# Merge, router norm and gate of a graph-attention router moved into the dense experts' program

## What is computed

```python
h = (x_flat @ W_gat).reshape(M, HEADS, NUM_EXPERTS)
a_src = (h * att_src).sum(-1)
a_dst = (h * att_dst).sum(-1)
e = jax.nn.leaky_relu(a_src[src] + a_dst[dst], negative_slope=0.2)
e_max = jax.ops.segment_max(e, dst, num_segments=M)
ee = jnp.exp(e - e_max[dst])
denom = jax.ops.segment_sum(ee, dst, num_segments=M)
alpha = ee / (denom[dst] + 1e-16)
msg = h[src] * alpha[:, :, None]
agg = jax.ops.segment_sum(msg, dst, num_segments=M).reshape(M, HEADS * NUM_EXPERTS) + b_gat
scores = _layernorm(agg, ln_gamma, ln_beta).reshape(M, HEADS, NUM_EXPERTS).mean(1)
topk_s, topk_i = jax.lax.top_k(scores, TOP_K)
w = jax.nn.softmax(topk_s, axis=-1)
for ei in range(NUM_EXPERTS):
    g = jnp.where(topk_i == ei, w, 0.0).sum(-1)
    hh = jax.nn.gelu(x @ W1[ei] + b1[ei], approximate=False)
    out = out + g[..., None] * (hh @ W2[ei] + b2[ei])
```

## Time and profile before

| what | us |
|---|---|
| median of 3 runs | 3600.15 (3591.07 to 3607.87) |
| span of the profiled execution, first to last instruction | 3135.8 |
| last copy of a dense output starts | 1534.97 |
| first VectorE instruction of the merge that needs own | 1582.93 |
| merge's last multiplies start | 1595.23 |
| router norm starts | 1602.31 |
| gate starts | 1610.19 |
| gate's last instruction starts | 1615.35 |

### The profile page before, as it was taken

One profiled execution on the slowest core, in us unless ns is written; L12 is line 12 of the kernel. 1 busy time (PEld: TensorE's weight loads), 2 busy tenths in 40 slices (PEclk: granted clock), 3 DMA queues, 4 the chain that ended last, 5 costly groups with the idle time before them and its releaser, 6 DMA issues. The chain is left out here.

```text
span 3135.8 us, 49560 instructions
## 1 busy us (share of the span) xinstructions
PE 2277.1 (73%) x10753; PEld 1712.5 (55%) x10754; DVE 1912.2 (61%) x4728; ACT 843.3 (27%) x2017; POOL 1501.4 (48%) x1250
## 2 busy tenths in 40 slices
PE   3677778777773789999637688887887755049973
PEld 2455556555552567777524455555555534049961
DVE  5646787767776533332467488788888844334437
ACT  0111222222120422222211355455555401013320
POOL 0487888888884027771110366556666400430023
PEclk7667787778775879999858899899999966579985
DMA  7566777777776224221234555555555416212233
GB/s 251 128 95 111 118 119 125 120 125 120 114 118 129 100 75 145 66 61 36 76 118 140 163 164 162 151 162 163 163 162 162 125 47 234 83 61 70 70 121 92
DMA packets 265541, 379.89 MB, mean 121 GB/s; under 512 B 36827, under 2 KB 197491, under 8 KB 265331
## 3 DMA queue, kind: packets, MB, share of 16 engines
q0 software_dynamic: 108320, 187.88, 30.3%
q1 hardware_dynamic: 135795, 151.42, 15.8%
q10 hardware_dynamic: 21344, 39.59, 3.5%
HBM read 247.23 MB, written 131.54 MB: 121 GB/s over the span
## 5 line engine op out<-in xcount | busy, mean ns | idle before, releaser
L1150 POOL DMA_INDIRECT sum_tab<-Vs,spot x416 | 707.7, 1701 | 180.3 <-issue 100.3
L2570 POOL DMA_INDIRECT KV<-kv_tab,iS x448 | 443.1, 989 | 217.1 <-issue 137.7
L1056 PE MATMUL psV<-XN,Bs 128*128 x832 | 323.8, 503 | 162.6 <-issue 134.5
L1056 PEld LDWEIGHTS psV<-XN,Bs 128*128 128x128 f32 x832 | 162.5, 235 | 293.5 <-issue 286.0
L2734 PE MATMUL psQ<-Qs,hotT 128*128 x904 | 249.0, 423 | 20.2 <-issue 11.5
L2745 PE MATMUL psO<-msg,hot 128*128 128x264 f32 x896 | 239.2, 413 | 17.8 <-issue 8.7
L1125 ACT COPY Vs<-psV 128x512 f32<-128x512 f32 x208 | 121.7, 585 | 472.8 <-DMA sum_tab<-Vs,spot 377.7
L2734 PEld LDWEIGHTS psQ<-Qs,hotT 128*128 128x128 f32 x904 | 169.8, 204 | 83.3 <-issue 57.6
L1673 POOL DMA_INDIRECT ST<-h_tab,src x192 | 182.9, 953 | 58.5 <-issue 58.5
L2745 PEld LDWEIGHTS psO<-msg,hot 128*128 128x128 f32 x896 | 169.7, 199 | 64.0 <-issue 26.9
L1794 PE MATMUL psY<-W2s,hT 128*128 128x256 f32 x800 | 184.3, 380 | 0.0
(11 more groups left out here) (570 smaller groups left out, 4389.8 us busy)
## 6 DMA issues: line engine op xcount, KB each, us to landing
kb<-key_rows SPq DMA_DIRECT2D x104, 256.0 KB, 3.9
sum_tab<-zeros ACTq DMA_DIRECT2D x52, 256.0 KB, 3.0
parts<-sum_tab SPq DMA_DIRECT2D x20, 640.0 KB, 8.6
ye_tab<-Ye SPq DMA_DIRECT2D x20, 640.0 KB, 3.7
Y<-ye_tab SPq DMA_DIRECT2D x20, 640.0 KB, 8.7
disp_tab<-AE ACTq DMA_DIRECT2D x10, 896.0 KB, 4.8
lowB<-sort_tab SPq DMA_DIRECT2D x23, 384.0 KB, 6.4
xb<-disp_tab SPq DMA_DIRECT2D x68, 128.0 KB, 2.1
```

The lines of the kernel that those rows point to most:

```text
L1056: ins = nc.tensor.matmul(psV[:, r % 2, x, :], Bs[:, q % 2, 2 * h + x, :], XN[:, bass.ds(t, 1), :].rearrange("p a d -> p (a d)"), start=Tru ...
L1150: pool.indirect_dma_start(out=sum_tabs[k], out_offset=bass.IndirectOffsetOnAxis(ap=spot[:, s, u:u + 1], axis=0), in_=Vs[:, j % VR, :], in_ ...
L2570: pool.indirect_dma_start(out=KV[:, s, u, :], out_offset=None, in_=kv_tab, in_offset=bass.IndirectOffsetOnAxis(ap=iS[:, s, u:u + 1], axis= ...
```

## The change

merge_phase and router_phase go, and the first layer calls gate_phase no more. Their work stands in gat_phase, in the same program as the dense steps:

- ScalarE does the exponential of AE behind the copies of step 13 instead of 16; that of tw between gelu(17) and the copies of step 16; that of wts behind the copies of step 18; root and last exponential behind step 19.
- TensorE spreads the tails behind down(15) and does all 25 tail products behind down(16), into the two banks of psL, with one signal at the end.
- GpSimd, and no longer SyncE, writes ST to gat_tab as soon as states is signalled, then gathers own.
- VectorE makes all 25 one-hots in one instruction early in the phase, takes tails straight from ST, spreads the four heads in one add and one reduce, and blends by head (4 times 100 elements) rather than by tile (25 times 16).
- The parameter rows and the row of -BIG for nodes without edges are loaded and stored early, on SyncE.

```diff
-        def merge_phase(H, F, tails, cont, endrow, table, agg, self_score=None, self_rows=None, eps=None):
...
-        EXP_AT = STEPS - 4
+        STATES_AT, SPREAD_AT, TAILS_AT, OTHERS_AT, BLEND_AT = STEPS - 7, STEPS - 5, STEPS - 4, STEPS - 4, STEPS - 2
...
-        def gat_phase(HG, self_score, XNT, b1T, tails):
+        def gat_phase(HG, XNT, b1T, cont, endrow, G):
...
+                tails, sq = ST[:, NJ2 - 1, :], prod
...
+                        pool.wait_ge(states, 1)
+                        pool.dma_start(gat_tab[0:E2, :].rearrange("(p j) w -> p j w", j=NJ2), ST[:, :, :]).then_inc(stored, 16)
+                        pool.wait_ge(z_stored, 16)
+                        pool.wait_ge(stored, 16)
+                        for t in range(NT):
+                            pool.indirect_dma_start(out=own[:, t, :], out_offset=None, in_=gat_tab,
+                                                    in_offset=bass.IndirectOffsetOnAxis(ap=endrow[:, t:t + 1], axis=0)).then_inc(own_in, 16)
...
+                        c.inc(v.memset(zrow[:, H:W], 0.0))
+                        c.inc(v.memset(zrow[:, 0:H], -BIG))
                         c.seq(v.tensor_single_scalar(highi[:, :], src2[:, :], 7, ALU.logical_shift_right))
+                        dve.sem_inc(z_ready, 1)
...
+                        c.seq(v.tensor_scalar(cm[:, :], iota_free[:, 0:NT], -float(P), cont[:, :], ALU.mult, ALU.add))
+                        c.seq(v.tensor_tensor(oh[:, :, :], iota_free[:, :].unsqueeze(1).broadcast_to([P, NT, P]),
+                                              cm[:, :].unsqueeze(2).broadcast_to([P, NT, P]), ALU.is_equal))
...
-                        c.seq(v.tensor_copy(tails[:, :], ST[:, NJ2 - 1, :]))
                         dve.sem_inc(states, 1)
...
+                        for h in range(H):
+                            c.inc(v.tensor_scalar(diag[:, h, :], ident[:, :], tails[:, h:h + 1], None, ALU.mult))
+                        c.inc(v.tensor_scalar(diag[:, H, :], ident[:, :], cont[:, :], None, ALU.mult))
+                        c.wait()
+                        dve.sem_inc(diags, 1)
+                        dve.wait_ge(spread, 1)
...
+                        dve.sem_inc(targ, 1)
+                        c.inc(v.tensor_scalar(tw_rows[:, 0:H], ref[:, :], lead[:, :], None, ALU.mult))
...
+                        dve.wait_ge(texp, 1)
...
+                        dve.sem_inc(rows_tw, 1)
+                        dve.wait_ge(others, 1)
...
+                        c.seq(v.tensor_tensor(oR, oR, has.broadcast_to([P, NT, H]), ALU.add))
+                        c.seq(v.tensor_tensor(top_[:, :, :], oR, self_score[:, :, :], ALU.max))
+                        dve.wait_ge(own_in, 16 * NT)
...
+                        dve.sem_inc(warg, 1)
+                        dve.wait_ge(prm_in, 48)
+                        dve.wait_ge(wexp, 1)
...
+                        for h in range(H):
+                            c.inc(v.tensor_tensor(by_head(own, 2 * H, h), by_head(own, 2 * H, h), share(0, h), ALU.mult))
+                            c.inc(v.tensor_tensor(by_head(other, 2 * H, h), by_head(other, 2 * H, h), share(1, h), ALU.mult))
+                            c.inc(v.tensor_tensor(by_head(agg, 0, h), by_head(HG, A0, h), share(2, h), ALU.mult))
+                        c.wait()
...
+                        c.seq(v.tensor_tensor(own[:, :, 2 * H:W], own[:, :, 2 * H:W], other[:, :, 2 * H:W], ALU.add))
+                        c.inc(v.reciprocal(den[:, :, :], den[:, :, :]))
+                        c.seq(v.tensor_tensor(agg[:, :, :], own[:, :, 2 * H:W], agg[:, :, :], ALU.add))
+                        for h in range(H):
+                            c.inc(v.tensor_tensor(by_head(agg, 0, h), by_head(agg, 0, h), den[:, :, h:h + 1].broadcast_to([P, NT, C]), ALU.mult))
+                        c.wait()
...
+                        dve.sem_inc(vars_, 1)
+                        dve.wait_ge(rooted, 1)
...
+                        dve.sem_inc(garg, 1)
+                        dve.wait_ge(gexp, 1)
...
+                        c.seq(v.tensor_tensor(G[:, :, :].rearrange("p e t -> p t e"), mask[0][:, :, :], mask[1][:, :, :], ALU.add))
...
+                        def spread_tails():
+                            pe.wait_ge(weighed, NLU)
+                            pe.wait_ge(diags, 1)
+                            nc.tensor.matmul(psL[:, 0, 0:4 * P], ones[:, :], diag[:, 0:4, :].rearrange("p h c -> p (h c)"), start=True, stop=True)
+                            nc.tensor.matmul(psL[:, 1, 0:P], ones[:, :], diag[:, H, :], start=True, stop=True).then_inc(spread, 1)
+
+                        def take_others():
+                            pe.wait_ge(targ, 1)
+                            pe.wait_ge(rows_tw, 1)
+                            for t in range(NT):
+                                at = t % OB * CW
+                                ins = nc.tensor.matmul(psL[:, t // OB, at:at + CW], oh[:, t, :], tw_rows[:, :], start=True, stop=True)
+                            ins.then_inc(others, 1)
...
                             down(n)
+                            if n == SPREAD_AT:
+                                spread_tails()
+                            if n == OTHERS_AT:
+                                take_others()
...
+                        act.wait_ge(nulled, 1)
...
-                        act.wait_ge(nulled, 1)
...
                                 gelu(n + 1)
+                            if n == TAILS_AT:
+
+                                act.wait_ge(targ, 1)
+                                a.activation(tw[:, :], tw[:, :], ACT.Exp).then_inc(texp, 1)
...
                             for t in range(GT):
                                 act.wait_ge(rows_out, n * GT + t + 1)
                                 a.copy(Ye[:, n % 2, t, :], psY[:, (n * GT + t) % 2, 0:D]).then_inc(rows_read, 1)
-                            if n == EXP_AT:
+                            if n == STATES_AT:
 
                                 act.wait_ge(args, 1)
                                 flat = AE[:, :, :, :].rearrange("p n h j -> p (n h j)")
                                 a.activation(flat, flat, ACT.Exp).then_inc(exps, 1)
+                            if n == BLEND_AT:
+
+                                act.wait_ge(warg, 1)
+                                flat = wts[:, :, :, :].rearrange("p n t h -> p (n t h)")
+                                a.activation(flat, flat, ACT.Exp).then_inc(wexp, 1)
                         act.wait_ge(blanked, 16 * len(pieces))
+                        act.wait_ge(vars_, 1)
+                        a.activation(var[:, :], var[:, :], ACT.Sqrt, bias=eps_col[:, :], scale=1.0 / F).then_inc(rooted, 1)
+                        act.wait_ge(garg, 1)
+                        a.activation(e2[:, :], e2[:, :], ACT.Exp).then_inc(gexp, 1)
...
                         sp.dma_start(table_rows(h_tab), HG[:, :, :]).then_inc(tabled, 16)
+                        for n, dr in enumerate((f0_bgat, f0_lng, f0_lnb)):
+                            sp.dma_start(prm[:, n, :], dr.partition_broadcast(P)).then_inc(prm_in, 16)
+                        sp.wait_ge(z_ready, 1)
+                        sp.dma_start(gat_tab[E2:E2 + 1, :], zrow[:, :]).then_inc(z_stored, 16)
...
-                        sp.wait_ge(states, 1)
-                        sp.dma_start(gat_tab[0:E2, :].rearrange("(p j) w -> p j w", j=NJ2), ST[:, :, :]).then_inc(stored, 16)
-                        sp.wait_ge(stored, 16)
...
-        def router_phase(agg, SC):
...
-                    gat_phase(HG, self_score, XNT0, b1T0, tails0)
-                    merge_phase(4, 16, tails0[:, :], cont2, end2, gat_tab, agg0, self_score[:, :, :], HG[:, :, 8:24], 1e-16)
-                    router_phase(agg0, SC0)
-                    gate_phase(SC0, E0, G0)
+                    gat_phase(HG, XNT0, b1T0, cont2, end2, G0)
```

More of the change, by code:

```diff
@@ new lines, in _ @@
+                        dve.sem_inc(rows_tw, 1)
+                        dve.wait_ge(others, 1)
+                        for b in range(2):
+                            ts = slice(b * OB, min((b + 1) * OB, NT))
+                            c.inc(v.tensor_copy(other[:, ts, :].rearrange("p t w -> p (t w)"), psL[:, b, 0:(ts.stop - ts.start) * CW]))
+                        c.wait()
+                        oR = other[:, :, 0:H]
+                        has = other[:, :, CW - 1:CW]
+                        c.seq(v.tensor_scalar(has, has, 1.0, BIG, ALU.subtract, ALU.mult))
@@ new lines, in _ @@
+                        c.seq(v.tensor_tensor(e2[:, :], m_[:, 1, :], m_[:, 0, :], ALU.subtract))
+                        dve.sem_inc(garg, 1)
+                        dve.wait_ge(gexp, 1)
+                        c.seq(v.tensor_scalar(gw[:, 0, :], e2[:, :], 1.0, None, ALU.add))
+                        c.seq(v.reciprocal(gw[:, 0, :], gw[:, 0, :]))
+                        c.seq(v.tensor_tensor(gw[:, 1, :], gw[:, 0, :], e2[:, :], ALU.mult))
+                        for n in range(2):
```

(1 more changed line is left out.)

238 lines of the change are left out of this document (67 added, 171 removed).

## The result

| | before | after |
|---|---|---|
| median, us (runs) | 3603.29 (4 runs, 3591.07 to 3607.87) | 3550.30 (4 runs, 3545.93 to 3553.88) |
| span of the profiled execution | 3135.8 | 3552.1 |

The ratio is 0.984, with a 95% interval of 0.9813 to 0.9868: 53 us faster, 48 to 67 by the interval. The forecast was a gain of 59.3 us and a time of 3541, with a range of 3528 to 3556. In a second series (e10) the changed kernel took 3557.77 against 3612.52, ratio 0.9858 (0.9834 to 0.9883), 54.8 us.

A forecast was written before the change was run, and what follows sets the result against it. It took the serial chain of 80.3 us behind step 19's last copy as the target; gate's end moves from 1615.7 to 1529.6 + O + 19.8 = 1556.4, a gain of 59.3, so 3600.15 - 59.3 = 3541 us, range 3528 to 3556.

The forecast's parts named there:

- a chain of 80.3 us: Step 19's last copy to gate's end: write, 25 gathers, vector work, program changes; all but 13 us go under the steps.
- The 464.35 us between them: Gap between the span of 3135.8 us and the median of 3600.15 us, taken as fixed time outside the instructions.
- O: What the 25 tail products (50 passes) behind down(16) cost TensorE, taken as 7 us, mostly at full clock.
- VectorE behind wexp: Time at which the exponential of wts behind step 18's copies is handed to VectorE: 1529.6 + O = 1536.6.
- rest of the blend: VectorE's blending after the exponential of wts: 6.1 us, or 2.1 more if the 16 by-head operations do not overlap.
- wexp to gate's end: VectorE's closing chain after the exponential of wts: rest of the blend, norm, root and gate, 19.8 us in sum.
- slow write: Rival: GpSimd's write of ST takes 44 us, so the end comes 10 us later; 3549 to 3555 us, chance 0.08.
- Missed slots: Rival: args or a tail slot comes late and TensorE pays; 3543 to 3549 us, 0.23 together with half clock throughout.
- Half clock throughout: Rival: the tail products run wholly at half clock; 3543 to 3549 us, chance 0.23 together with missed slots.
- The slower case: Rival: GpSimd writes ST in pieces of 24 floats, 243 us, end 150 us later, 3750 us; chance 0.02.
- the work does not move: Rival: some wait chains the new vector work behind step 19; no effect, chance 0.02.
- TensorE idles in the steps: Sign in the dense steps that the prediction is wrong; they were to stay at 17.25 us each.

The follow-up runs named there:

- e10: Changed kernel run again unchanged, beside the kernel before: 3557.77 us against 3612.52, ratio 0.9858.
- e3: Changed kernel with the 25 gathers of own replaced by one direct load of the same bytes: 3523.57 us, ratio 0.9784 to the kernel before.
- e11: Changed kernel with the 218 early indirect DMAs in bursts of 8 and the merge behind step 19, second run: 3405.41 us against 3612.52 before, ratio 0.9438.
- e6: Changed kernel with the 25 gathers of own issued in four bursts (6, 6, 6, 7): 3515.86 us against 3583.10 before, ratio 0.9798.
- e12: Changed kernel with early indirect DMAs in bursts of 8 and own's gathers in four bursts, AE's exponential behind step 13: 3132.66 us against 3137.60 before, ratio 0.9983.
- e2: Changed kernel with the 25 gathers of own started only after the tail products: 3551.33 us, ratio 0.9854 to the kernel before.
- e7: Changed kernel with own's 25 gathers replaced by 25 direct loads from SyncE behind its store of step 15: 3505.43 us against 3583.10 before, ratio 0.9772.
- e9: Changed kernel with the 218 early indirect DMAs in bursts of 8 and the merge behind step 19, first run: 3149.20 us against 3137.00 before, ratio 1.0033.
- e4: Changed kernel with the 25 small tail products replaced by two wide ones, gathers kept: 3546.16 us, ratio 0.9832 to the kernel before.
- e8: Changed kernel with the 192 early gathers of source rows replaced by 12 direct loads on the same queue: 3290.52 us, in one run.

## Why the prediction was right, and where it was not

The mechanism forecast, a chain of 80.3 us of which all but 13 goes under the steps, is there: 13.0 remain. The total is in the range too, but that is luck in part: two steps were wrong, with opposite signs, and their errors of 14.6 and 20.0 us nearly cancel.

**"The 464.35 us between them lie outside the instructions; I take them as fixed."** They lie inside: 265 ahead of the gate's end, 199 behind it. They are not fixed either, for most of them follow GpSimd's gathers, and the change moves 25 of those. The first trace showed a merge of before without the stall, where the timed runs had one of 14.6 us more. Alone, this made the gain larger than worked out.

**O, taken as 7.** The 7 was my choice, and no run shows it; what the runs showed in its place is 7.6 without the stall (e3: 5.74 us of passes, and 1.9 more behind them, most of it from the clock of 0.50) and 10.84 for the passes alone at 0.50 (e11). The sum adds O in full to the end, and that held: the earlier trace rows have TensorE busy 50.00 of 50.00 us at 1.00 in the dense steps, and in after VectorE resumed behind wexp 27.6 us later, all that TensorE lost. Steps 16 and 17 of after take 39.40 and 23.80 us instead of 18.33 (17.25 and the spread) and 17.25, so TensorE lost 39.40 + 23.80 - 18.33 - 17.25 = 27.6 us there. Of that the products are 7.6 (e3) and the stall, with the lower clock in it, 20.0. The size of the products was right; what failed is that their neighbour was not asked for. The gathers stood in the sum only as a chain of their own, to be hidden.

Together: 59.3 + 14.6 - 20.0 - 0.6 = 53.3, against 53.2 in the stretch. Were both kernels free of the stall, the gain in the stretch would be, by my estimate from e3 and e6, about 177.3 - 118.7 = 58.6; no series showed after itself so, and e3, e6 and e12 only come near.

Point by point, after's times less the 247.87 us by which its step 13 ends later (1686.59 and 1438.72):

| step | forecast | measured |
|---|---|---|
| states ready | 1466.5 | 1466.4 |
| write by GpSimd | about 12 | 11.2 |
| first gather of own | 1479 | 1478.6 |
| spread on TensorE | 1.1 | 1.1 |
| tail products, O | 7 | 7.6, with the stall 27.6 |
| VectorE behind wexp | 1529.6 + O | 1557.3 = 1529.7 + 27.6 |
| rest of the blend | 6.1 | 5.93 |
| wexp to gate's end | 19.8 | 19.7 |
| last copy to gate's end | 13 | 13.0 |

**The rivals.** The slow write did not come: it took 11.2 us. Missed slots: none; VectorE's last instruction for args (L1619) ended 1.9 us ahead of the end of step 13's last copy, and the load of the Gelu table behind the products stays hidden (in e3 TensorE is busy for 1.93 of the 2.00 us beside it). The by-head operations overlap, 0.17 us apart. "Half clock throughout" took place in after, where TensorE ran thinly (15.25 of 27.00 us busy, at 0.50), but as a result of the stall; in e3 the products ran at 1.00 and 0.99. Behind them, though, TensorE was busy 3.00 of 3.00 us at 0.50. All 50 passes at half clock do occur, in e11, where TensorE had stood nearly idle since the last step: 10.84 us, where fifty passes at the 0.213 us of the earlier trace rows make 10.7. Being busy did not keep the clock up in e3: the passes took 5.74 us at full clock and the slow spell behind them, with TensorE busy throughout, 1.9 more. The earlier trace rows had shown the like, 3.70 of 3.70 us busy at 0.50. The slower case and "the work does not move" are out.

Of the prediction's own signs of failure one appeared, "TensorE idles in the steps", and by that sign the prediction failed in O although its total held. It was the right thing to watch.

**What stays open** is how GpSimd's gathers hold the others up. In after each single instruction waits (1.40 us between a weight load and its product, 22.4 and 28.0 us between ScalarE's). That what the engines lack is instructions, as the theories of e2 and e7 have it, was my guess, and no trace or run shows it. Nor did one show why two series had no stall, or why the 416 indirect DMAs ahead of the dense steps cause none.

## What to carry to other kernels

Hold the span of the trace against the times of the runs before any sum; where they differ by 13%, the trace is of another regime. Its rows then price what is alike in both, as most steps here were, but not what runs beside GpSimd's gathers. When work is moved under a cover, ask what else runs beside it: a chain that is itself hidden, as these gathers were, can hold up the engine that hides it. On runs like these, issue indirect DMAs of GpSimd in bursts: 6 to 12 with pauses of 8 to 10 us between cost nothing, and e6 is 20 us shorter in the stretch than the changed kernel by that alone. Bursts of 8 for the early ones, with pauses of 2 us, gained 152 us over the changed kernel in their series (e11 against e10), although the later merge makes e11's stretch 49 us longer. Where the stall is absent such bursts gain nothing (e9 and e12).

## What the runs showed of the hardware

- In four series of six, rows of GpSimd's indirect DMAs (128 rows of 96 bytes, 1.255 us apart) all but stopped the other engines: 20 to 21 us for 25 of them wherever other work stood beside them (e2, e4, after, e10), and some 242 for 192 (e8, one run). The first ten (TensorE's first stop in after, 12.6 us in) to 12 (in a row in e6, stretch 118.7) cost nothing; in the long row of after ScalarE then starts a copy every 28.0 us or a gelu every 22.4, and TensorE's load and product start 1.40 us apart.
- With next to nothing beside them the same 25 cost nothing (e11 against e9: 188.2 and 188.0 us).
- Waiting for 8 to land before the next 8, a pause of mostly 2 us, left 67 us (e11) of the 255 that after loses from its first copy to step 2 (306.1, where the first trace has 50.8).
- 25 direct loads of the same shape from SyncE, 0.47 us apart, cost nothing (e7, stretch 118.6 as in e3).
- In such a stretch TensorE's clock falls as well, to a mean of 0.56 from 1200 to 1440 us in after.
- Fifty passes of 25 columns took 5.74 us at full clock (e3) and 10.84 at half (e11). At the end of those of e3 the granted clock fell to 0.50 for 3.4 us, and of those of e12 for 6.8, though TensorE was never idle in either.
